# Slot arithmetic and two convolution additions placed on GpSimd in a Mamba-2 and mixture-of-experts kernel

## The chip, the cores and the metric

The kernel runs on one core of one Trainium2 chip. The metric is device time in microseconds from start to end of one execution; smaller is better.

## The reference

The input is x, 16 sequences of 512 tokens of 128 values, f32. The layer has two halves. The first is a Mamba-2 block: a projection of each token into z (256), xBC (512) and dt (4), a causal convolution with four taps over each of the 512 xBC channels, silu, and a scan in which a state of 4 heads x 64 x 128 is decayed and added to at each token. Its output is normalised by its root mean square, gated by silu(z), projected back to 128, added to x and layer-normalised. The second half is a mixture of 8 experts with the top 2 per token, again with residual and layer norm. Cut to what the change touches:

```python
xBC = conv1d(xBC, conv_w, 4 taps, causal) + conv_b     # each channel by itself
xBC = silu(xBC)                                        # 256 x channels, 128 B, 128 C
...
gates = sigmoid(u @ centroids.T); topk_vals, topk_idx = top_k(gates, 2)
gates = mask / sum(mask)
out = einsum('ne,end->nd', gates, outs)                # outs: each token by each expert
x = layernorm(x + out)
```

The kernel computes only the two chosen experts of a token. For that each token's row is written twice to a list in HBM that is sorted by expert.

## The kernel before, in words

The program has three stages. In the first the 16 sequences are walked in slots, written out one after another (`slots`, k from -1 to 16). In slot s the engines do three sequences at once: the scan of s, the projection and convolution of q = s+1, and the routing of r = s-1; the rows of s-2 are scattered to the list. A slot goes through four chunks c = 0..3 of 128 tokens. The second stage runs 136 tiles of 128 sorted rows through the experts, the third adds the two rows of each token and normalises. The order on each engine is the order of the code in `slot_pe`, `slot_act`, `slot_dve` and `slot_pool`; no scheduler moves anything, and each engine takes its instructions strictly in order, with semaphores between engines.

What matters in a slot, by engine and line:

- TensorE (`slot_pe`): per chunk the exponents (L420 to L425, into `pl`), transposes of xc (L518, L520), the state product (L524), a projection block for q (L399), the y products (L542, L548) and the new state (L556). In chunk 1 `turn_parts` (L412) and the transposes of the routed rows (L566). Behind the chunks: z, the sums of squares (L585), then the output product (L593), which waits for all four gated chunks (`g_ready`), the products of B and C (L496), z again (L407), the ranks (L609 to L613).
- ScalarE (`slot_act`): exponentials (L688), the copy `Btok` (L798), the convolution's newest tap with its bias (`tap0`, L730, into `acc`), in chunk 1 the normalised rows (L810), then `cur` (L719), `S` (L725, `keep_parts`), a square (L783) and the copy `uT` (L822). At the end silu of the four `acc` blocks (`activate`, L736).
- VectorE (`slot_dve`): `Xdt` (L1091), the statistics and `ve` (L1054), `carried`, `shift` (L1103), the masked `M` (L998), `yv` (L1117), `state` (L1122, L1125), and the other three taps of each of the four convolution blocks (`tap`, L924: acc += weight * shifted projection, read from PSUM). `take_ranks` and `place_rows` (L1002 to L1028) turn ranks into slot numbers: the product of picks and rows, its sum over 8 experts, the two gate values, two token numbers, a cast, and the next token numbers. They write the last two columns of `rowA` and `rowB`.
- GpSimd (`slot_pool`): `Xdd` (L1379), `decayed` (L1373), the gated chunk `gt` (`gate_y`, L1359), two powers (`rstd` L1394, `rms` L1415), and the eight indirect DMAs that scatter the rows of s-2 (L1366, four for `rowA`, four for `rowB`). Of the `rowA` scatters two stand behind gate_y(1), two behind gate_y(2); the four of `rowB` stand behind `rms`.

Waits of the lines quoted in the change: `Xdt` of chunk c < 3 waits for `Btok` of the same chunk; L556 waits for `Xdd`; L566 waits for `S` and for L810; L593 waits for gate_y(3).

Of the kernel before, what the change touches and what calls it, by code (L numbers as in the profile page):

```python
# [27 lines left out]
P = 128  # L28
# [20 lines left out]
G0 = 2  # L49
Q = 32  # L50
KS = 3 * Q
NH = NC * H
POS_STEPS = 4
# [24 lines left out]
def build(nc, t, out):  # L78
    ctx = ExitStack()
    with ctx:  # L80
# [6 lines left out]
        def sem(name):  # L87
# [31 lines left out]
        token_id = sb("token_id", [P, NC])  # L119
# [7 lines left out]
        acc = sb("acc", [P, XC, TOKS])  # L127
        xc = [sb(f"xc{i}", [P, XC, TOKS]) for i in range(2)]
# [33 lines left out]
        rowA = [sb(f"rowA{i}", [P, NC, ROW]) for i in range(2)]  # L162
        rowB = [sb(f"rowB{i}", [P, NC, ROW]) for i in range(2)]
# [11 lines left out]
        slotf = sb("slotf", [P, NC, 2])  # L175
# [34 lines left out]
              for big in (acc, xc[0]) for i in range(2)]  # L210
# [44 lines left out]
        names_pool = ("picks_made", "Xdd_ready", "decayed_ready", "g_ready", "rms_ready", "rstd_ready")
        (picks_made, Xdd_ready, decayed_ready, g_ready, rms_ready, rstd_ready) = [sem(n) for n in names_pool]
# [136 lines left out]
        def _(pe):  # L393
            def project_block(q, k):
                if k == 0:
                    wait(pe, sz_ready, CC * (q.n - 1) + 1)
                else:
                    wait(pe, conv_done, XC * q.n + k - 1)
                pe.matmul(pj[k % 2][:, :], w_xbc[:, k * P:(k + 1) * P], xT[:, q.n, :],  # L399
                          start=True, stop=True).then_inc(proj_psum, 1)  # L400

            def z_block(q, k):
                if k > 0:
                    wait(pe, carried_ready, (NC - 1) * q.n)
                else:
                    pe.wait_ge(conv_done, XC * q.n + 3)
# [93 lines left out]
            def slot_pe(s, scan, project, route):  # L500
# [4 lines left out]
                for c in range(NC):  # L505
                    tok = slice(c * P, (c + 1) * P)
                    n = NC * s.n + c
                    if scan and (c + 1 < NC or project):
# [26 lines left out]
                    if scan:  # L535
# [140 lines left out]
        def _(act):  # L676
# [50 lines left out]
            def tap0(q, c):  # L727
# [58 lines left out]
            def slot_act(s, scan, project, route):  # L786
# [4 lines left out]
                for c in range(NC):  # L791
# [94 lines left out]
        def _(dve):  # L886
# [115 lines left out]
            def take_ranks(r):  # L1002

                dve.wait_ge(rank_psum, r.n + 1)
                dve.tensor_tensor(rows[:, :, :], p4[:, 0:NC * E].rearrange("p (c e) -> p c e", e=E),
# [5 lines left out]

            def place_rows(r):

                link = chain(pos_step, POS_STEPS * r.n + 1)
                dve.wait_ge(rank_read, r.n + 1)
                dve.wait_ge(rowB_ready, r.n + 1)
                dve.reciprocal(gsum[:, :], gsum[:, :])
                link(dve.tensor_tensor(prow[:, :, :, :], picks[:, :, :, :],
                                       rows[:, :, :].unsqueeze(2).broadcast_to([P, NC, 2, E]), ALU.mult))
                link(dve.tensor_reduce(slotf[:, :, :], prow[:, :, :, :], AX_X, ALU.add))  # L1020
                for row, k in ((rowA, 0), (rowB, 1)):
                    dve.scalar_tensor_tensor(out=row[r.par][:, :, P + 1], in0=top[:, :, k], scalar=2.0,
                                             in1=gsum[:, :], op0=ALU.mult, op1=ALU.mult)
                    dve.tensor_scalar(row[r.par][:, :, P].bitcast(I32), token_id[:, :],
                                      float(TOKENS * k), None, ALU.add)
                link(dve.tensor_copy(slot[r.par][:, :, :], slotf[:, :, :]))
                dve.tensor_scalar(token_id[:, :], token_id[:, :], float(TOKS), None,
                                  ALU.add).then_inc(slot_ready, 1)  # L1028
# [27 lines left out]
            def slot_dve(s, scan, project, route):  # L1056
# [24 lines left out]
                for c in range(NC):  # L1081
# [50 lines left out]
                    if c == 1 and not (isinstance(s.n, int) and s.n < 2):  # L1132
                        place_rows(s.plus(-2))
# [9 lines left out]
                if route:  # L1143
# [4 lines left out]
                    wait_apart(dve, gate_step, gate + 2)  # L1148
                    for k in range(NC):
# [7 lines left out]
                if route:  # L1157
# [7 lines left out]
                    wait(dve, slot_ready, r.n)  # L1165
# [333 lines left out]
```

## Time and profile before

| | us |
|---|---|
| median of 3 runs (lowest, highest) | 817.68 (816.87, 819.04) |
| the profiled execution's own time | 816.69 |
| span of its instructions | 814.9 |
| busy: TensorE matmul | 667.5 |
| busy: VectorE | 617.5 |
| busy: ScalarE | 475.8 |
| busy: GpSimd | 433.0 |

How to read it: the span is shorter than the time by what lies around the first and the last instruction. Busy shares are means over the three stages. The walk over the sequences ends at about 450 us, the expert stage runs from about 480 to 780 us, the last stage fills the rest.

### The profile page before, as it was taken

How to read it: one execution, taken by the hardware profiler on the slowest of the kernel's cores; microseconds unless marked ns; L12 is line 12 of the kernel's file. 1: busy time of each engine (PE TensorE's matmuls, PEld its weight loads, DVE VectorE, ACT ScalarE, POOL GpSimd, SP SyncE). 2: the span in 40 equal slices, each digit the busy share in tenths (PEclk: the TensorE clock that was granted, in tenths of full speed). 3: DMA queues.
4: the chain of work that ended last, by engine and by line, in shares of the span. 5: the costliest groups of instructions: out<-in, count | busy, mean ns of one | idle time of the engine just before them, and what ended most of it. 6: DMA issues, size and time to landing. Idle time of an engine off the chain costs nothing.

```text
span 814.9 us, 21092 instructions
## 1 busy us (share of the span) xinstructions
PE 667.5 (82%) x5092; PEld 546.9 (67%) x5093; DVE 617.5 (76%) x2128; ACT 475.8 (58%) x1179; POOL 433.0 (53%) x498
## 2 busy tenths in 40 slices
PE   7969999888898898988987139999999999999300
PEld 5846666566665566655665129999999999999300
DVE  4398989889999899998896536666667666667485
ACT  3737766676766767667673115555555555556165
POOL 4023265656656566565756634555555555555464
PEclk9999999999999999999999559999999999999755
DMA  9160010111101111011100122222222222222496
GB/s 258 33 229 14 15 41 14 37 30 40 41 14 37 31 40 37 18 33 34 41 20 24 57 60 57 66 63 65 64 65 65 65 63 64 65 64 70 108 311 203
DMA packets 74801, 54.09 MB, mean 66 GB/s; under 512 B 9435, under 2 KB 70110, under 8 KB 74480
## 3 DMA queue, kind: packets, MB, share of 16 engines
q1 hardware_dynamic: 56400, 31.90, 14.9%
q0 software_dynamic: 8448, 16.93, 6.3%
q10 hardware_dynamic: 9888, 4.49, 2.0%
q8 instruction: 29, 0.48, 0.3%
q14 instruction: 36, 0.29, 0.1%
HBM read 31.11 MB, written 22.69 MB: 66 GB/s over the span
## 4 chain that ended last, share of the span: by engine, by line
PE 71%; issue 9%; ACT 7%; DVE 5%; POOL 3%; DMA 2%; ACTq 1%; SPq 1%; DVEq 0%; POOLq 0%
PE pl L633 16%; PE p L645 14%; PE pj L399 5%; PE p L585 4%; PE p L593 3%; PE p L542 3%; PE p L548 2%; PE pj L627 2%; ACT rowA L810 2%; ACT sz L872 2%; POOL sorted_rows L1366 2%; PE pj L407 2%; PE p L556 2%; PE p L496 2%; PE p L407 2%
## 5 line engine op out<-in xcount | busy, mean ns | idle before, releaser
L851 ACT ACTIVATE L<-pl,b_sb 128x128 f32<-128x128 f32 x544 | 155.4, 369 | 118.1 <-PE pl L633 118.1
L1428 POOL DMA_INDIRECT moe_rows<-yv,xs x136 | 145.7, 1072 | 140.5 <-DVE yv L1235 124.1
L633 PE MATMUL pl<-Btok,M 128*128 128x128 f32 x1088 | 151.7, 283 | 1.2 <-DVE M L1223 0.7
L924 DVE SCALAR_TENSOR_TENSOR acc<-pj,conv_w_sb,acc 128x511 f32<-128x511 f32 (+2 forms) x192 | 142.7, 743 | 4.0 <-ACT acc L730 1.1
L645 PE MATMUL p<-w,L 128*128 x1088 | 143.9, 275 | 1.3 <-ACT L L851 1.3
L633 PEld LDWEIGHTS pl<-Btok,M 128*128 128x128 f32 x1088 | 133.7, 193 | 4.3 <-DVE M L1223 1.4
L645 PEld LDWEIGHTS p<-w,L 128*128 128x128 f32 x1088 | 132.4, 192 | 1.8 <-issue 1.8
L1219 DVE COPY Btok<-pj 128x128 f32<-128x128 f32 x136 | 39.7, 292 | 78.2 <-PE pl L633 63.2
L1379 POOL TENSOR_TENSOR Xdd<-Xdt,cur 128x256 f32<-128x256 f32 x48 | 29.5, 615 | 88.0 <-DVE Xdt L1091 80.1
L1366 POOL DMA_INDIRECT sorted_rows<-rowA,slot x64 | 64.7, 1011 | 19.1 <-issue 17.0
L1366 POOL DMA_INDIRECT sorted_rows<-rowB,slot x64 | 62.7, 980 | 18.0 <-issue 18.0
L730 ACT ACTIVATE acc<-pj,conv_b_sb,conv_w_sb 128x512 f32<-128x512 f32 x64 | 49.5, 773 | 35.4 <-PE pj L399 35.3
L399 PE MATMUL pj<-xT,w_xbc 128*128 128x512 f32 x128 | 66.5, 601 | 0.0
L542 PEld LDWEIGHTS p<-M,Xdt 128*64 128x64 f32 x512 | 27.3, 136 | 52.5 <-issue 48.9
L627 PE MATMUL pj<-ident,xs 128*128 128x128 f32 x136 | 39.9, 294 | 23.3 <-DMA xs<-sorted_rows 20.8
L1223 DVE COPY M<-w 128x512 f32 x136 | 57.0, 419 | 0.0
L688 ACT ACTIVATE pl<-pl 128x512 f32<-128x512 f32 x64 | 37.3, 582 | 33.8 <-PE pl L425 33.2
L1359 POOL TENSOR_TENSOR gt<-yv,sz 128x256 f32<-128x256 f32 x64 | 47.0, 734 | 11.3 <-DVE yv L1117 10.6
L1235 DVE SCALAR_TENSOR_TENSOR yv<-yv,xs 128x128 f32<-128x128 f32 x136 | 47.8, 352 | 4.8
L1232 DVE TENSOR_TENSOR yv<-p,b2e_mem 128x128 f32<-128x128 f32 x136 | 39.5, 291 | 15.2 <-PE p L645 8.9
L542 PE MATMUL p<-M,Xdt 128*64 128x128 f32 x512 | 42.1, 284 | 9.5 <-issue 6.8
L998 DVE TENSOR_TENSOR M<-pl,Gm 128x512 f32<-128x512 f32 x64 | 43.8, 685 | 2.0 <-ACT pl L688 1.4
(204 smaller groups left out, 1341.7 us busy)
## 6 DMA issues: line engine op xcount, KB each, us to landing
xs<-sorted_rows SPq DMA_DIRECT2D x136, 65.0 KB, 1.8
xres<-in_x SPq DMA_DIRECT2D x16, 256.0 KB
w<-in_w SPq DMA_DIRECT2D x2, 2048.0 KB, 10.2
acc<-moe_rows SPq DMA_DIRECT2D x16, 256.0 KB, 4.2
xc<-moe_rows SPq DMA_DIRECT2D x16, 256.0 KB, 5.0
out<-sz ACTq DMA_DIRECT2D x16, 256.0 KB, 4.6
moe_rows<-yv,xs POOLq DMA_INDIRECT x136, 2.4
xc<-in_x SPq DMA_DIRECT2D x4, 256.0 KB, 5.1
```

Source lines behind the costliest of these rows:

```text
L399: pe.matmul(pj[k % 2][:, :], w_xbc[:, k * P:(k + 1) * P], xT[:, q.n, :], start=True, stop=True).then_inc(proj_psum, 1)
L542: mm = pe.matmul(p7[half, (h // 2) * P:(h // 2 + 1) * P], Xdt[c % 2][:, h * HD:(h + 1) * HD], M[c % 2][:, h, :], start=(h < 2), stop=(c == ...
L627: pe.transpose(pj[k % 2][:, 0:P], xs[k][:, 0:P], ident[:, :]).then_inc(sT_psum, 1)
L633: mm = pe.matmul(pl[k % 2][:, f * P:(f + 1) * P], w1e[k % 2][:, f * P:(f + 1) * P], sT[k % 2][:, :], start=True, stop=True)
L645: mm = pe.matmul(o[:, 0:P], hT[k % 2][:, f, :], w2[:, bass.ds(e, 1), f, :].rearrange("p e d -> p (e d)"), start=(f == 0), stop=(f == FB - 1))
L730: act.activation(acc[:, c, :], pj[c % 2][:, :], ACT.Identity, bias=conv_b[:, c:c + 1], scale=conv_w[:, c, TAPS - 1:TAPS]).then_inc(tap0_do ...
L851: act.activation(hT[k % 2][:, f, :], pl[k % 2][:, f * P:(f + 1) * P], ACT.Gelu, bias=b1[:, bass.ds(e * FB + f, 1)]).then_inc(hT_ready, 1)
L924: ins = dve.scalar_tensor_tensor(out=acc[:, k, j:TOKS], in0=pj[k % 2][:, 0:TOKS - j], scalar=conv_w[:, k, TAPS - 1 - j:TAPS - j], in1=acc[ ...
L1223: dve.tensor_copy(w1e[k % 2], w1[:, bass.ds(e, 1), :].rearrange("p e f -> p (e f)")).then_inc(w1e_ready, 1)
L1235: dve.scalar_tensor_tensor(out=ye[k % 4], in0=ye[k % 4], scalar=xs[k][:, P + 1:P + 2], in1=xs[k][:, 0:P], op0=ALU.mult, op1=ALU.add).then_ ...
L1366: pool.indirect_dma_start(out=sorted_rows[:, :], out_offset=bass.IndirectOffsetOnAxis(slot[q.par][:, c, k:k + 1], 0), in_=(rowA, rowB)[k][ ...
L1428: pool.indirect_dma_start(out=moe_rows[:, :], out_offset=bass.IndirectOffsetOnAxis(xs[k][:, P:P + 1].bitcast(I32), 0), in_=ye[k % 4], in_o ...
```

## The change

Five edits:

1. `place_rows` moves from VectorE to GpSimd. It becomes nine GpSimd instructions: twice the sum `gain`, the product of picks and rows, the sum over 8 experts as three halving additions (`half`), one product that writes both gate columns, one cast that writes both token columns, the cast to `slot`, and the next token numbers. `rowA` and `rowB` become the halves of one tensor `pair`. The reciprocal of `gsum` goes to `take_ranks`, which stays on VectorE.
2. For the two x blocks of the convolution (k < 2) the oldest tap leaves VectorE: ScalarE writes the product to `oldest[k]` right behind `tap0` (128x509), GpSimd adds it to `acc` (`add_oldest`, 128x509). `activate` of these blocks waits for the addition.
3. GpSimd's order in a slot: `place_rows(s-2)` stands behind gate_y(0), the first `rowA` scatter behind decay_state(2), `add_oldest(0)` and the other three `rowA` scatters behind gate_y(1), `add_oldest(1)` and the first `rowB` scatter behind gate_y(2), the other three `rowB` scatters behind `rms`.
4. On ScalarE `keep_parts` (S) moves ahead of the normalised rows in chunk 1, `set_current` (cur) to chunk 3.
5. On TensorE the exponents of chunk 2 move from the start of chunk 1 to a place ahead of the state product of chunk 0, behind its waits for `Btok` and `Xdd`.

```diff
@@ slot_pe
-                    if scan and (c + 1 < NC or project):
+                    if scan and c != 1 and (c + 1 < NC or project):
...
                             pe.wait_ge(Xdd_ready, (NC - 1) * s.n + c + 1)
                             if c == 0:
+                                exponents(s, 2)
                                 pe.wait_ge(sz_ready, CC * (s.n + 1))
@@ tap0
+                if c < BY_POOL:
+                    wait(act, oldest_added, BY_POOL * (q.n - 1) + c + 1)
+                    act.activation(oldest[c][:, TAPS - 1:TOKS], pj[c % 2][:, 0:TOKS - TAPS + 1], ACT.Identity,
+                                   scale=conv_w[:, c, 0:1]).then_inc(tap3_done, 1)
@@ slot_act
+                    if project and c == 1:
+                        keep_parts(q, p4[0:KS, 0:P])
...
-                    if project and c == 1:
+                    if project and c == 3:
                         set_current(q)
-                        keep_parts(q, p4[0:KS, 0:P])
@@ tap
+                on_dve = TAPS - 1 - (k < BY_POOL)
+                if j > on_dve:
+                    return
...
                 if j == 1:
                     dve.wait_ge(tap0_done, XC * q.n + k + 1)
+                    if k < BY_POOL:
+                        dve.wait_ge(tap3_done, BY_POOL * q.n + k + 1)
@@ on GpSimd
+            def place_rows(r):
...
+                pool.wait_ge(rows_ready, r.n + 1)
...
+                pool.tensor_tensor(gain[:, :], gsum[:, :], gsum[:, :], ALU.add)
+                link(pool.tensor_tensor(prow[:, :, :, :], picks[:, :, :, :],
+                                        rows[:, :, :].unsqueeze(2).broadcast_to([P, NC, 2, E]), ALU.mult))
+                part = prow
+                for k in range(3):
+                    w = E >> (k + 1)
+                    if k == 1:
+                        pool.tensor_tensor(pair[r.par][:, :, :, P + 1], top[:, :, 0:2].rearrange("p c k -> p k c"),
+                                           gain[:, :].unsqueeze(1).broadcast_to([P, 2, NC]), ALU.mult)
+                    if k == 2:
+                        pool.tensor_copy(pair[r.par][:, :, :, P].bitcast(I32), token_id[:, :, :])
+                    link(pool.tensor_tensor(half[k][:, :, :, :], part[:, :, :, 0:w], part[:, :, :, w:2 * w],
+                                            ALU.add))
+                    part = half[k]
+                link(pool.tensor_copy(slot[r.par][:, :, :], half[2][:, :, :, 0]))
+                pool.tensor_scalar(token_id[:, :, :], token_id[:, :, :], 1.0, float(TOKS), ALU.mult,
+                                   ALU.add).then_inc(slot_ready, 1)
+
+            def add_oldest(q, k):
+                pool.wait_ge(tap3_done, BY_POOL * q.n + k + 1)
+                pool.wait_ge(taps_read, XC * q.n + k + 1)
+                pool.tensor_tensor(acc[:, k, TAPS - 1:TOKS], acc[:, k, TAPS - 1:TOKS], oldest[k][:, TAPS - 1:TOKS],
+                                   ALU.add).then_inc(oldest_added, 1)
```

How the order moves, at three places of a slot in the middle of the walk. First GpSimd from `Xdd` of chunk 2 to the scatters behind `rms`, before:

```order
L1379 TENSOR_TENSOR Xdd<-Xdt,cur 128x256
L1359 TENSOR_TENSOR gt<-yv,sz 128x2x128
L1366 DMA sorted_rows<-rowA,slot 67584x130 x2
L1359 TENSOR_TENSOR gt<-yv,sz 128x2x128
L1366 DMA sorted_rows<-rowA,slot 67584x130 x2
L1359 TENSOR_TENSOR gt<-yv,sz 128x2x128
L1415 TENSOR_TENSOR rms<-ms,neg_half 128x4
L1366 DMA sorted_rows<-rowB,slot 67584x130 x4
```

and of the changed kernel:

```order
L1415 TENSOR_TENSOR Xdd<-Xdt,cur 128x256
L1359 TENSOR_TENSOR gt<-yv,sz 128x2x128
L1395 TENSOR_TENSOR acc<-acc,oldest 128x509
L1402 DMA sorted_rows<-pair,slot 67584x130 x3
L1359 TENSOR_TENSOR gt<-yv,sz 128x2x128
L1395 TENSOR_TENSOR acc<-acc,oldest 128x509
L1402 DMA sorted_rows<-pair,slot 67584x130
L1359 TENSOR_TENSOR gt<-yv,sz 128x2x128
L1462 TENSOR_TENSOR rms<-ms,neg_half 128x4
L1402 DMA sorted_rows<-pair,slot 67584x130 x3
```

Ahead of the last `gt` four scatters stand as before, in runs of three and one, and two additions are new.

Second, ScalarE from `Btok` of chunk 1 to `Btok` of chunk 2, before:

```order
L798 COPY Btok<-p 128x128
L810 ACTIVATE rowA<-rowA,shift,rstd 128x128 x4
L730 ACTIVATE acc<-pj,conv_b_sb,conv_w_sb 128x512
L719 COPY cur<-vals 128x80
L725 CAST S<-p 96x128
L783 ACTIVATE ysq<-yv 128x2x128
L822 COPY uT<-p 128x512
L688 ACTIVATE pl<-pl 128x512
L798 COPY Btok<-p 128x128
```

and of the changed kernel:

```order
L811 COPY Btok<-p 128x128
L731 CAST S<-p 96x128
L825 ACTIVATE pair<-pair,shift,rstd 128x128 x4
L736 ACTIVATE acc<-pj,conv_b_sb,conv_w_sb 128x512
L740 ACTIVATE oldest<-pj,conv_w_sb 128x509
L796 ACTIVATE ysq<-yv 128x2x128
L836 COPY uT<-p 128x512
L694 ACTIVATE pl<-pl 128x512
L811 COPY Btok<-p 128x128
```

`S` stands ahead of the four normalised rows, `cur` is gone from here, and one product is new.

Third, TensorE at the end of chunk 0, before:

```order
L542 MATMUL p<-M,Xdt 64x128 x4
L556 MATMUL p<-Xdd,Btok 128x256
L420 MATMUL pl<-too_early,ident_b 128x512
L422 MATMUL pl<-pick_s,S 128x512
L425 MATMUL pl<-S,pick_t 128x128 x4
L518 MATMUL p<-ident,xc 128x128 x2
```

and of the changed kernel:

```order
L547 MATMUL p<-M,Xdt 64x128 x4
L425 MATMUL pl<-too_early,ident_b 128x512
L427 MATMUL pl<-pick_s,S 128x512
L430 MATMUL pl<-S,pick_t 128x128 x4
L562 MATMUL p<-Xdd,Btok 128x256
L523 MATMUL p<-ident,xc 128x128 x2
```

The exponents of chunk 2 (`pl`) and the state product change places.

## Rows read from the trace of the kernel before

**Rows 1.** Windows view, a stretch of the walk: length; busy PE, PEld, DVE, ACT, POOL; clock.

```profile
136.00:300.00 164.00, 145.92 (x1038) 102.11 (x1037) 148.37 (x489) 113.83 (x220) 101.98 (x122) 1.00 0.12 34
```

**Rows 2.** Chain that ended last, pieces in order of time: start us, us, what.

```profile
54.22 0.67 DVE acc L924
...
248.21 1.32 issue
249.53 0.67 PE p L556 x2
```

**Rows 3.** Timeline of VectorE: start us, us, engine, line, what, idle before.

```profile
93.91 0.42 DVE L1091 TENSOR_TENSOR Xdt<-p,cur 128x256 f32<-128x256 f32 x1 [0.26 <-ACT Btok L798]
...
118.94 0.42 DVE L1091 TENSOR_TENSOR Xdt<-p,cur 128x256 f32<-128x256 f32 x1 [0.56 <-ACT Btok L798]
...
232.25 0.42 DVE L1091 TENSOR_TENSOR Xdt<-p,cur 128x256 f32<-128x256 f32 x1 [0.41 <-issue]
...
246.98 0.42 DVE L1091 TENSOR_TENSOR Xdt<-p,cur 128x256 f32<-128x256 f32 x1 [0.55 <-ACT Btok L798]
...
248.85 0.62 DVE L1054 TENSOR_SCALAR ve<-mv 128x4 f32<-128x4 f32 x1
...
257.86 0.42 DVE L1091 TENSOR_TENSOR Xdt<-p,cur 128x256 f32<-128x256 f32 x1 [0.41 <-issue]
...
426.89 0.42 DVE L1091 TENSOR_TENSOR Xdt<-p,cur 128x256 f32<-128x256 f32 x1 [0.56 <-ACT Btok L798]
...
428.61 0.17 DVE L1054 TENSOR_SCALAR ve<-mv 128x4 f32<-128x4 f32 x1
```

**Rows 4.** Timeline of GpSimd.

```profile
233.32 0.73 POOL L1359 TENSOR_TENSOR gt<-yv,sz 128x256 f32<-128x256 f32 x1
234.22 1.06 POOL L1366 DMA_INDIRECT sorted_rows<-rowA,slot  x1 [0.17 <-issue]
...
236.56 0.73 POOL L1359 TENSOR_TENSOR gt<-yv,sz 128x256 f32<-128x256 f32 x1
...
239.76 0.73 POOL L1359 TENSOR_TENSOR gt<-yv,sz 128x256 f32<-128x256 f32 x1
...
243.94 1.06 POOL L1366 DMA_INDIRECT sorted_rows<-rowB,slot  x1 [0.20 <-issue]
...
248.80 0.62 POOL L1379 TENSOR_TENSOR Xdd<-Xdt,cur 128x256 f32<-128x256 f32 x1
...
255.66 0.61 POOL L1373 TENSOR_TENSOR decayed<-state,cur 128x256 f32<-128x256 f32 x1 [2.11 <-DVE state L1125]
258.36 0.61 POOL L1379 TENSOR_TENSOR Xdd<-Xdt,cur 128x256 f32<-128x256 f32 x1 [2.09 <-DVE Xdt L1091]
...
454.49 1.03 POOL L1366 DMA_INDIRECT sorted_rows<-rowA,slot  x1 [2.14 <-DVE token_id L1027]
```

**Rows 5.** Timeline of TensorE, the output product.

```profile
241.74 1.98 PE L593 MATMUL p<-w_out,gt 128*128 128x128 f32 x16
```

**Rows 6.** Timeline of ScalarE, chunk 1 to chunk 2.

```profile
252.92 1.65 ACT L810 ACTIVATE rowA<-rowA,shift,rstd 128x128 f32<-128x128 f32 x4 [1.26 <-DVE shift L1103]
254.47 0.76 ACT L730 ACTIVATE acc<-pj,conv_b_sb,conv_w_sb 128x512 f32<-128x512 f32 x1
255.13 0.24 ACT L719 COPY cur<-vals 128x80 f32<-128x80 f32 x1
...
255.44 0.42 ACT L783 ACTIVATE ysq<-yv 128x256 f32<-128x256 f32 x1
256.40 0.59 ACT L822 COPY uT<-p 128x512 f32<-128x512 f32 x1 [0.55 <-PE p L566]
...
257.50 0.27 ACT L798 COPY Btok<-p 128x128 f32<-128x128 f32 x1
```

**Rows 7.** Groups of GpSimd instructions by shape: xcount, busy us, mean ns, idle before.

```profile
L1442 POOL TENSOR_TENSOR xc<-xc 128x128 f32<-128x128 f32 x8 | 3.6, 452 | 1.5 <-DMA xc<-moe_rows 0.8 <-ACT sz L872 0.7
...
L1347 POOL TENSOR_TENSOR which<-ident 96x16 f32<-96x16 f32 x1 | 0.2, 209 | 0.0
```

More of the change, by code:

```diff
@@ L49 @@
 G0 = 2
+BY_POOL = 2
 Q = 32
@@ L52 @@
 NH = NC * H
-POS_STEPS = 4
+POS_STEPS = 1
+PLACE_STEPS = 5
 FIN_STEPS = 3
@@ L127, in build @@
         acc = sb("acc", [P, XC, TOKS])
+        oldest = [sb(f"oldest{i}", [P, TOKS]) for i in range(BY_POOL)]
         xc = [sb(f"xc{i}", [P, XC, TOKS]) for i in range(2)]
@@ L161, in build @@
         shift = sb("shift", [P, NC])
-        rowA = [sb(f"rowA{i}", [P, NC, ROW]) for i in range(2)]
-        rowB = [sb(f"rowB{i}", [P, NC, ROW]) for i in range(2)]
+        pair = [sb(f"pair{i}", [P, 2, NC, ROW]) for i in range(2)]
+        rowA = [b[:, 0] for b in pair]
+        rowB = [b[:, 1] for b in pair]
         uT = sb("uT", [P, TOKS])
@@ L174, in build @@
         prow = sb("prow", [P, NC, 2, E])
-        slotf = sb("slotf", [P, NC, 2])
+        half = [sb(f"half{i}", [P, NC, 2, E >> (i + 1)]) for i in range(3)]
+        gain = sb("gain", [P, NC])
         slot = [sb(f"slot{i}", [P, NC, 2], I32) for i in range(2)]
@@ L397, in project_block @@
                 else:
-                    wait(pe, conv_done, XC * q.n + k - 1)
+                    wait(pe, taps_read, XC * q.n + k - 1)
                 pe.matmul(pj[k % 2][:, :], w_xbc[:, k * P:(k + 1) * P], xT[:, q.n, :],
@@ L1004, in take_ranks @@
                 dve.wait_ge(rank_psum, r.n + 1)
+                wait(dve, slot_ready, r.n)
                 dve.tensor_tensor(rows[:, :, :], p4[:, 0:NC * E].rearrange("p (c e) -> p c e", e=E),
@@ L1010, in take_ranks @@
                                   ALU.add).then_inc(rank_read, 1)
[L1012 to L1028, printed above, removed]
+                dve.reciprocal(gsum[:, :], gsum[:, :]).then_inc(rows_ready, 1)
             def residual(s):
@@ L1148, in slot_dve @@
                     wait_apart(dve, gate_step, gate + 2)
+                    wait(dve, slot_ready, r.n)
                     for k in range(NC):
@@ L1175, in _ @@
             take_ranks(Seq(0, SEQS - 1))
-            place_rows(Seq(0, SEQS - 1))
             link = chain(table_step, 0)
@@ L1387, in slot_pool @@
                     make_picks()
+                    for k in range(BY_POOL):
+                        add_oldest(q, k)
                     return
@@ L1398, in slot_pool @@
                     gate_y(s, 0)
+                if scatters:
+                    place_rows(old)
+                if scan:
                     decay_state(s, 2)
+                if scatters:
+                    scatter(old, 0, 0)
+                if scan:
                     decay_x(s, 2)
                     gate_y(s, 1)
+                if project:
+                    add_oldest(q, 0)
                 if scatters:
-                    scatter(old, 0, 0)
-                    scatter(old, 1, 0)
+                    for c in range(1, NC):
+                        scatter(old, c, 0)
                 if scan:
                     gate_y(s, 2)
+                if project:
+                    add_oldest(q, 1)
                 if scatters:
-                    scatter(old, 2, 0)
-                    scatter(old, 3, 0)
+                    scatter(old, 0, 1)
                 if scan:
@@ L1416, in slot_pool @@
                 if scatters:
-                    for c in range(NC):
+                    for c in range(1, NC):
                         scatter(old, c, 1)
             slots(pool, slot_pool)
+            place_rows(Seq(0, SEQS - 1))
             for k in range(2):
```

43 lines of the change are left out of this document (25 added, 18 removed).

## The prediction

> **What bounds the kernel now.** I read the windows view first. In a stretch in the middle of the walk VectorE is busy for 148.4 of 164 us and TensorE for 145.9, ScalarE for 113.8, GpSimd for 102.0, all at the full clock [rows 1]. So two engines are near their limit, GpSimd looks free, and the sum of busy time can't say more. The chain of waits then shows where TensorE stands still: 1.32 us before the state product of chunk 0 [rows 2], which waits for `Xdd`. GpSimd starts that `Xdd` at 248.80 only because the four `rowB` scatters that began at 243.94 stand ahead of it [rows 4]; `Xdt` was there at 247.40 [rows 3]. A second stop, from the end of the y products of chunk 1 to the transposes of the routed rows, ends with `S`, which stands on ScalarE behind the four normalised rows, the tap and `cur` [rows 6].
>
> Last I cut one period into three pieces, since a share over a slot hides who waits. The marks are `Xdt` of chunk 2 (232.25), the output product (241.74), `Xdt` of chunk 0 (246.98) and `Xdt` of chunk 2 again (257.86) [rows 3, 5]. B, from `Xdt` 2 to the output product, is 9.49 us; C, from there to `Xdt` 0, is 5.24; A, from `Xdt` 0 to `Xdt` 2, is 10.88. Together 25.61. From 118.94 to 426.89 there are 12 such periods, 25.66 on average [rows 3].
>
> **Piece A: a gain of 0.7 us.** With one of the four `rowB` scatters gone from ahead of it, `Xdd` 0 is ready 1.26 us earlier (four scatters take 4.86 from 243.94 to 248.80, the first 1.06 + 0.30 [rows 4]); so it no longer runs beside `ve`, which took 0.62 us in that company (248.85) and 0.17 in a slot where `Xdd` came a little later (428.61) [rows 3, 4]. The state product is also early enough. What VectorE does next in order, up to `shift`, comes 0.5 us earlier, less 0.08 for the reciprocal: 0.42. `S` and the exponents of chunk 2 then stand ahead of their users and cost nothing. ScalarE goes on behind `shift`: from the normalised rows (252.92) to `Btok` 2 (257.50) it now takes 4.58 us [rows 6]. The spacing behind `tap0` is 0.66 (254.47 to 255.13), and the new product, of the same form, adds this much. `cur` and `S` give back 0.31 (255.13 to 255.44). The copy `uT` came 0.96 after the square because the transposes were late (0.55 idle) [rows 6]; back to back it comes 0.31 after, so 0.65 more is saved. 4.58 + 0.66 - 0.31 - 0.65 = 4.28. Piece A: 10.88 - 0.42 - 0.30 = 10.16. The taps and the slot arithmetic that leave VectorE (about 2.5 us a slot) give nothing more here, since `Xdt` 2 waits for `Btok` 2 and the cover is ScalarE.
>
> GpSimd must still have `Xdd` 2 ready. Between gate_y(0) and `Xdd` 2 it has now 2.11 + 2.09 us idle [rows 4]; 0.3 of this goes, as piece A is shortened more at its end than at `shift`. `place_rows` goes in: nine instructions. The nearest row is 209 ns for 16 elements [rows 7]; with the slope below the nine take 1.9 us, and about 0.1 us at each of four waits on itself makes 2.3. The scatter that also goes in takes 1.25. 3.55 against 3.9: hidden, with only 0.35 us to spare. The low end of its cost is nothing; at the high end, if halving with short inner runs costs twice as much for each, it takes 3.5 and adds 0.85 us to each slot.
>
> **Piece B: a loss of 1.35 us.** Here GpSimd is given work on its only tight stretch. Before: `Xdd` 2 starts 0.50 us behind `Xdt` 2 (257.86 to 258.36), then gate_y(1), two scatters, gate_y(2), two scatters, gate_y(3), which ends at 240.49, 8.24 us behind `Xdt` 2, with no gap above 0.30 [rows 4]. The output product needs gate_y(3), and starts 1.25 us later [rows 5]. In the new order there are again four scatters in this stretch, and two additions of 128x509 besides. No row shows such an addition. The rows give 452 ns for 128x128 [rows 7] and 730 for 128x256 [rows 4]: 2.2 ns an element, so 1.29 us for 509. The low end comes from `Xdd` (615 ns, one operand repeated) and the 16-element row, 1.7 ns an element and 1.04 us; the high end adds 10% for strides, 1.42. I take 1.29, since both its rows have two full operands. Each addition overlaps its neighbour by 0.04, so the two take 2.50; gate_y(3) ends 10.74 behind `Xdt` 2, and the output product starts at 10.84 instead of 9.49. TensorE's own work would have let it start at 9.3.
>
> [...]
>
> **Piece C** keeps its order and its 5.24 us: the three `rowB` scatters left behind `rms` end 1 us before the next `Xdd`.
>
> A period: 10.16 + 10.84 + 5.24 = 26.24, 0.63 more than 25.61.
>
> **The sum.** Slots 3 to 14: 12 x 0.63 = +7.6. Slot 2 has scatters of `rowA` but none of `rowB` left over, and lasts 25.03 (93.91 to 118.94) [rows 3]; it goes to 26.24: +1.2. Slot 1 has no scatters, so GpSimd hides everything: 0. Slot 0 is carried by VectorE with its softplus steps between the taps (its tap on the chain costs 0.67 [rows 2]); two taps go: -1.3. In the startup ScalarE's new products stand ahead of copies that TensorE waits for; between nothing and one product of 0.7, and I take the latter: +0.7. At the end: slot 15 has no additions and keeps the 0.7 of piece A as a gain; behind its `rms` GpSimd carries the chain to its last scatter. One scatter has moved ahead (-1.26), the wait of 2.14 us for VectorE's slot arithmetic [rows 4] goes, and `place_rows` stands in twice, 2 x 2.45: together +1.5, less 0.7: +0.8. The table of tiles is built on VectorE beside the last eight scatters, as before. The expert stage and the last one hold no edited line. 7.6 + 1.2 - 1.3 + 0.7 + 0.8 = +9.0 us.
>
> The profiled execution took 816.69 us, so 825.7 for one like it. The median of the runs shown is 1.0 above it, so I predict 826.7.
>
> **Rivals.** (1) VectorE is the bound, and taking 2.5 us a slot from it counts. For it: 90% busy. Against it: piece B, where GpSimd had 1.25 us to spare and gets 2.5 us more. It decides where an addition takes under 0.9 us; then B is left to TensorE at 9.3, a period is 24.7, and 12 x -0.9 with slot 2 at -0.3 gives -11.1 + 0.2 from the ends: 807. Chance 0.12. (2) The additions take 1.04 us: each period is 0.5 shorter, 13 of them 6.5, and the time is 820; with a little more gain in piece A it can't be told from before. Chance 0.15. (3) `place_rows` takes 3.5 us or more on GpSimd: `Xdd` 2 is late by 0.85, and 13 slots give +11, the end +2: 840. The count of nine chained instructions speaks for it, the 209 ns row against it. Chance 0.13. My forecast keeps 0.60.
>
> **How the numbers follow.** A measurement of this kernel can tell 0.3%, 2.45 us, from no change. Within the forecast, additions of 1.42 us add 3.4, a `place_rows` of 3 us adds 6, and 0.35 us a slot more gain in piece A takes 4.5 off: 822 to 834. The range reaches down to 816, over rival 2 with that same gain, and up to 839, most of the way to rival 3; rival 1 stays outside. Faster 0.12, same 0.15, slower 0.73 (forecast and rival 3).
>
> **What the profile would show.** Right: VectorE's busy time down by some 45 us (32 taps and 16 times the slot arithmetic) and GpSimd's up by about 70 (32 x 1.29 and 16 x 1.9); the group of the addition at 1.26 to 1.29 us x32; the output product idle before, put down to gate_y on GpSimd, about 1.5 us in 13 slots; no stop before the state product of chunk 0; the period between two `Xdt` of chunk 0 near 26.2. Wrong: an addition under 1 us; the last gate_y of a slot ending before the sums of squares do; `Xdt` 2 less than 9.8 or more than 10.6 behind `Xdt` 0, in which case piece A is misjudged, through ScalarE or through `place_rows`.

## The result, and the profile after

The changed kernel takes **824.34 us** (median of 4 runs, 824.15 to 824.6), the kernel before, run beside it, 817.27 (816.5 to 819.04). The ratio is 1.0084, with a 95% interval of 1.0066 to 1.0101: slower by 7 us. The profiled execution has a span of 822.8 us (814.9 before).

The page of the changed kernel, busy time by engine and the chain that ended last:

```profile
span 822.8 us, 21204 instructions
PE 679.5 (83%) x5092; PEld 552.0 (67%) x5093; DVE 580.4 (71%) x1968; ACT 491.2 (60%) x1211; POOL 503.4 (61%) x674
...
PE 49%; POOL 25%; issue 14%; DVE 4%; ACT 3%; DMA 2%; SPq 1%; ACTq 1%; DVEq 0%; POOLq 0%
```

VectorE is 37 us less busy (45 were forecast), GpSimd 70 more (as forecast), and GpSimd now holds 25% of the chain, 3% before. The windows view of the stretch that [rows 1] showed:

```profile
136.00:300.00 164.00, 147.31 (x1023) 102.08 (x1023) 130.67 (x418) 117.64 (x228) 128.63 (x189) 1.00 0.10 32
```

No engine is above 90% here (the row has TensorE, its weight loads, VectorE, ScalarE, GpSimd), and VectorE has lost 18 us of work. The waits of TensorE in the same stretch say what holds it (waiting instruction, releaser: us in total, times, longest):

```profile
PE p L599 <- POOL gt L1359: 8.3, 7, 1.2
PE p L572 <- ACT pair L825: 3.2, 6, 0.5
PE p L529 <- DVE state L1125: 2.4, 6, 0.4
```

The output product (now L599) waits 1.2 us in each slot for GpSimd's last gate_y. The stop of 1.32 us before the state product of chunk 0 is gone. GpSimd's timeline in the middle of the walk answers to [rows 4]:

```profile
234.86 0.60 POOL L1415 TENSOR_TENSOR Xdd<-Xdt,cur 128x256 f32<-128x256 f32 x1 [0.26 <-DVE Xdt L1094]
235.43 0.72 POOL L1359 TENSOR_TENSOR gt<-yv,sz 128x256 f32<-128x256 f32 x1
236.11 1.26 POOL L1395 TENSOR_TENSOR acc<-acc,oldest 128x509 f32<-128x509 f32 x1
237.53 1.02 POOL L1402 DMA_INDIRECT sorted_rows<-pair,slot  x1 [0.16 <-issue]
...
241.10 0.74 POOL L1359 TENSOR_TENSOR gt<-yv,sz 128x256 f32<-128x256 f32 x1
241.78 1.28 POOL L1395 TENSOR_TENSOR acc<-acc,oldest 128x509 f32<-128x509 f32 x1
243.23 1.01 POOL L1402 DMA_INDIRECT sorted_rows<-pair,slot  x1 [0.17 <-issue]
244.26 0.74 POOL L1359 TENSOR_TENSOR gt<-yv,sz 128x256 f32<-128x256 f32 x1
...
250.93 0.61 POOL L1415 TENSOR_TENSOR Xdd<-Xdt,cur 128x256 f32<-128x256 f32 x1 [1.17 <-issue]
```

From `Xdd` 2 to gate_y(3) it never rests: an addition, three scatters, gate_y(2), an addition, a scatter, gate_y(3). In front of the next `Xdd` 0 it then has 1.17 us to spare, where the kernel before had none.

The marks of one period, on VectorE and (last row) TensorE, answer to [rows 3, 5]:

```profile
234.34 0.42 DVE L1094 TENSOR_TENSOR Xdt<-p,cur 128x256 f32<-128x256 f32 x1 [0.69 <-ACT Btok L811]
...
250.37 0.43 DVE L1094 TENSOR_TENSOR Xdt<-p,cur 128x256 f32<-128x256 f32 x1 [0.78 <-ACT Btok L811]
...
260.21 0.42 DVE L1094 TENSOR_TENSOR Xdt<-p,cur 128x256 f32<-128x256 f32 x1 [0.69 <-ACT Btok L811]
```

```profile
245.05 2.05 PE L599 MATMUL p<-w_out,gt 128*128 128x128 f32 x16 [1.20 <-POOL gt L1359]
```

So B is 10.71 us (before 9.49), C 5.32 (5.24), A 9.84 (10.88): a period of 25.87 where it was 25.61. The change gave A one microsecond and took 1.2 from B.

### The profile page after: what moved, and what is told of

Same layout as the page of the kernel before. It is cut to its first block, busy times and chain, and to the rows that moved or that the text cites. A ratio compares the mean times of both kernels' runs of the same rounds, so it can differ in the third digit from the quotient of the medians.

```text
span 822.8 us, 21204 instructions
## 1 busy us (share of the span) xinstructions
PE 679.5 (83%) x5092; PEld 552.0 (67%) x5093; DVE 580.4 (71%) x1968; ACT 491.2 (60%) x1211; POOL 503.4 (61%) x674
## 4 chain that ended last, share of the span: by engine, by line
PE 49%; POOL 25%; issue 14%; DVE 4%; ACT 3%; DMA 2%; SPq 1%; ACTq 1%; DVEq 0%; POOLq 0%
PE pl L639 16%; PE p L651 15%; POOL sorted_rows L1402 10%; POOL gt L1359 4%; PE p L599 4%; POOL acc L1395 3%; PE pj L633 2%; POOL rstd L1432 2%; PE p L501 2%; PE p L412 2%; ACT sz L886 2%; PE pl L448 2%; DVE st L1050 1%; DMA acc<-moe_rows 1%; PE pj L404 1%
## 5 line engine op out<-in xcount | busy, mean ns | idle before, releaser
L1402 POOL DMA_INDIRECT sorted_rows<-pair,slot x128 | 128.3, 1003 | 34.9 <-issue 33.4
L943 DVE SCALAR_TENSOR_TENSOR acc<-pj,conv_w_sb,acc 128x511 f32<-128x511 f32 (+2 forms) x160 | 118.7, 742 | 19.0 <-ACT oldest L740 15.6
L1094 DVE TENSOR_TENSOR Xdt<-p,cur 128x256 f32<-128x256 f32 x64 | 27.0, 422 | 32.7 <-ACT Btok L811 22.7
L599 PE MATMUL p<-w_out,gt 128*128 128x128 f32 x256 | 32.7, 281 | 16.0 <-POOL gt L1359 16.0
```

Of the source, the lines that this page charges most:

```text
L599: mm = pe.matmul(p5[:, c * P:(c + 1) * P], gt[:, k, c * P:(c + 1) * P], w_out[:, k, :], start=(k == 0), stop=(k == CC - 1))
L943: ins = dve.scalar_tensor_tensor(out=acc[:, k, j:TOKS], in0=pj[k % 2][:, 0:TOKS - j], scalar=conv_w[:, k, TAPS - 1 - j:TAPS - j], in1=acc[ ...
L1402: pool.indirect_dma_start(out=sorted_rows[:, :], out_offset=bass.IndirectOffsetOnAxis(slot[q.par][:, c, k:k + 1], 0), in_=(rowA, rowB)[k][ ...
```

## The experiments

All were timed beside the kernel before, whose medians on those chips were 816.1 to 816.8 us; each ratio is against that median. Each kernel is judged by the pieces A, B and C, read in the middle of its walk from the same three marks. The figures together, in us:

| kernel | time | A | B | C | period |
|---|---|---|---|---|---|
| before | 816.4 | 10.88 | 9.49 | 5.24 | 25.61 |
| changed | 824.3 | 9.84 | 10.71 | 5.32 | 25.87 |
| 1 no additions | 797.3 | 9.32 | 9.50 | 5.24 | 24.05 |
| 2 first `rowB` scatter back | 820.7 | 10.85 | 9.45 | 5.31 | 25.62 |
| 3 a third addition | 843.2 | 9.84 | 11.70 | 5.32 | 26.85 |
| 4 place_rows on VectorE | 818.9 | 9.84 | 10.76 | 5.32 | 25.90 |
| 5 as 1 and 4 | 807.6 | 9.85 | 9.84 | 5.24 | 24.95 |
| 6 before, edits 4 and 5 | 813.4 | 10.85 | 9.34 | 5.24 | 25.44 |
| 7 one addition | 801.4 | 9.32 | 9.84 | 5.31 | 24.46 |
| 8 before, edit 1 | 843.0 | 10.92 | 10.75 | 5.32 | 26.98 |
| 9 as 1, scatters as before | 812.9 | 10.39 | 9.49 | 5.24 | 25.12 |
| 10 gate_y(3) first | 804.6 | 9.84 | 9.35 | 5.33 | 24.52 |
| 11 as 1, last places on VectorE | 793.5 | 9.32 | 9.50 | 5.24 | 24.05 |
| 12 as 11, exponents as before | 794.3 | 9.32 | 9.50 | 5.24 | 24.06 |

**1. No additions.** The oldest taps go back to VectorE; all else stays.

```diff
-BY_POOL = 2
+BY_POOL = 0
...
-                if project:
-                    add_oldest(q, 0)
...
-                if project:
-                    add_oldest(q, 1)
```

> The changed kernel with no oldest tap on GpSimd: all four convolution blocks keep three taps on VectorE, ScalarE writes no product, GpSimd adds none; everything else as changed. Theory G (the two additions of 1.27 us each stand between Xdt 2 and gate_y(3), and GpSimd sets the output product there): piece B falls from 10.71 to TensorE's own 9.3 to 9.5, piece A from 9.84 to about 9.5 (ScalarE 0.6 shorter), C stays 5.3; a period of 24.1 to 24.5, so 800 to 806 us in all. Rival V (VectorE is the bound, the two taps it gets back cost 1.4 us a slot): the period stays at 25.8 or rises, 824 us or more. Rival P (the slot arithmetic on GpSimd is what costs): no gain, 822 to 826.

Measured: 797.26 us, ratio 0.9769 (0.9753 to 0.9786). That is 3 us below the range expected: B is as expected, and A is 9.32 where 9.5 was. The other four edits make the kernel 19 us faster, and edit 1 takes 27 us away again. VectorE as the bound (rival V) is refuted, since it got work back and the kernel became faster. TensorE's output product no longer waits; TensorE and VectorE are both above 90% busy, in the windows view of this kernel:

```profile
136.00:300.00 164.00, 156.49 (x1102) 108.06 (x1100) 149.74 (x462) 118.01 (x232) 121.77 (x193) 1.00 0.12 35
```

A also fell, by 0.52, with the products gone from ScalarE.

**2. The first `rowB` scatter back behind `rms`.**

```diff
-                if scatters:
-                    scatter(old, 0, 1)
                 if scan:
                     gate_y(s, NC - 1)
...
-                    for c in range(1, NC):
+                    for c in range(NC):
                         scatter(old, c, 1)
```

> The changed kernel with one scatter moved: the first rowB scatter, which stands ahead of gate_y(3), goes back behind rms, so that four stand there. The same work on every engine. Theory G: gate_y(3) ends 1.23 us earlier, piece B is 9.5, the next Xdd 0 is at most 0.2 us late and still early enough for the exponents; a period of 24.6 and 13 slots give -15: 808 to 811 us. Rival X (the delay of Xdd behind four scatters, 1.3 us in the kernel before, comes back in full): the period stays near 25.8, 824 us.

Measured: 820.72 us, ratio 1.005 (1.0032 to 1.0068). B fell by 1.26, as the scatter's price says, and A rose by 1.01. GpSimd's timeline in this kernel:

```profile
243.70 1.04 POOL L1460 TENSOR_TENSOR rms<-ms,neg_half 128x4 f32<-128x4 f32 x1 [1.04 <-DVE ms L1157]
244.94 1.05 POOL L1402 DMA_INDIRECT sorted_rows<-pair,slot  x1 [0.20 <-issue]
...
248.82 0.96 POOL L1402 DMA_INDIRECT sorted_rows<-pair,slot  x1 [0.30 <-issue]
249.80 0.63 POOL L1415 TENSOR_TENSOR Xdd<-Xdt,cur 128x256 f32<-128x256 f32 x1
```

and TensorE's, which stands 1.27 us for that `Xdd` before the exponents of chunk 2:

```profile
250.53 0.38 PE L425 MATMUL pl<-too_early,ident_b 128*128 128x512 bf16 x1 [1.27 <-issue]
```

Once gate_y(3) is early, `rms` waits for `ms` instead, so the four scatters behind it end no sooner, and `Xdd` 0 is late again. The scatter costs about the same on either side. The expectation of 808 to 811 us, by which the place ahead of gate_y(3) was the dear one, failed.

**3. A third addition** ahead of gate_y(3), on tiles of its own.

```diff
                     add_oldest(q, 1)
+                    pool.tensor_tensor(idle_out[:, TAPS - 1:TOKS], idle_in[:, TAPS - 1:TOKS],
+                                       idle_in[:, TAPS - 1:TOKS], ALU.add)
```

> The changed kernel with a third, useless addition of 128x509 on GpSimd behind add_oldest(1), that is ahead of gate_y(3), on tiles of its own. Theory G: 1.23 us more in piece B in each of 13 slots, +16, 840 us; slots 0 and 1 hide it. A rival by which GpSimd is not what the output product waits for: under +5, below 829.

Measured: 843.19 us, ratio 1.0338 (1.0303 to 1.0373). B rises by 0.99: GpSimd's queue in this piece is the bound there. Over 13 slots that is 13 us of the 19. The rest is TensorE's clock. Five of the 13 slots take 28.2 to 28.6 us instead of 26.85, 7.4 us in all (startup, slot 0 and end give 1.2 back), and in each of the five the output product runs slow after its stop:

```profile
225.46 3.48 PE L601 MATMUL p<-w_out,gt 128*128 128x128 f32 x16 [2.19 <-POOL gt L1362]
```

against 2.05 us in the changed kernel; the window around it has this granted clock (the third figure from the end), partly at the lower level, 1.2 GHz. The other eight slots had the same stop (2.17 to 2.25 us) and kept the full clock:

```profile
225.00:229.00 4.00, 3.54 (x19) 3.54 (x20) 0.85 (x5) 1.40 (x3) 3.42 (x4) 0.57 0.10 33
```

**4. place_rows back on VectorE**, at the end of chunk 1, in the changed kernel.

```diff
-                if scatters:
-                    place_rows(old)
...
                         take_ranks(s.plus(-2))
+                    if c == 1 and not (isinstance(s.n, int) and s.n < 2):
+                        place_rows(s.plus(-2))
```

> The changed kernel with place_rows back on VectorE, at the end of chunk 1, where VectorE waits 1.1 us for ScalarE's product; additions, scatters and the order of ScalarE and TensorE as changed. Theory G: pieces A and B unchanged (the arithmetic was hidden on GpSimd and is hidden on VectorE), period 25.9; behind slot 15 two times 3.2 us of GpSimd's chain go and 2.1 us of waiting come back, -4: 819 to 821 us. Rival P (the arithmetic costs GpSimd's chain in the walk too): 0.3 us or more a slot besides, 816 or less. Rival V: VectorE's 1.2 us come back in each slot, 835 or more.

Measured: 818.93 us, ratio 1.0039 (1.0025 to 1.0053). The period moves by 0.03: on GpSimd place_rows was hidden. Of the 5.4 us that are gained 3.4 lie at the end. From `Xdt` of slot 15 to the first expert matmul it is 51.90 us, and 55.31 in the changed kernel. Another 1.8 lie at the start of the expert stage, where the clock came back sooner (see below); no run ties that to this edit.

**5. Both of these.** 

> The changed kernel without the additions (edit 1) and with place_rows back on VectorE (edit 2): edits 3 to 5 alone. What it leaves out: nothing. Theory G (GpSimd ahead of TensorE is what costs; without the additions GpSimd has room, so place_rows there costs the period nothing, but costs 2.2 us twice in the last two slots, where nothing else hides it): periods as in the kernel without the additions (24.06, within 0.2), and 3 to 5 us less behind slot 14, so 793 to 796 us against its 797.3. Rival V (VectorE has become the bound at a period of 24: the 1.6 us of place_rows and the place it takes behind the row products of chunk 1 are then paid in each slot): periods 24.5 to 25, 803 to 810 us.

Measured: 807.64 us, ratio 0.9884 (0.9859 to 0.9908); rival V. Without the additions VectorE has no room: place_rows there costs 0.90 us a slot, in A and in B. So edit 2 earns nothing in the period beside edit 1, and 0.90 without it.

**6. The kernel before with the two orders (edits 4 and 5) alone.** 

> The kernel before with edits 4 and 5 alone: ScalarE copies S to cur behind block 3 and the parts at chunk 1, TensorE's exponents of chunk 2 go behind the wait for the scaled rows. Computes the same. If the orders are what brought the period of the kernel without the additions from 25.6 to 24.06: 24.1 to 24.6 here, 798 to 804 us. If the rest of it was needed (place_rows off VectorE, the scatters in ones and threes), so that in the kernel before the exponents only fall behind GpSimd's scaled rows, late by the two scatters ahead of it: 25.0 to 25.5, 809 to 815 us. Rival X: the exponents' wait is worth more than the copy's move: 25.8 or more, over 818 us.

Measured: 813.4 us, ratio 0.9959 (0.9945 to 0.9974). The period falls by 0.17, to 25.44, the second of the three cases expected. A hardly moves: the late `Xdd` 0 now holds up the exponents of chunk 2, before which TensorE stands 1.32 us.

**7. One addition**, block 0's (`BY_POOL = 1`, and the second call of `add_oldest` taken out). 

> The changed kernel with one addition in place of two: block 0's stays on GpSimd, block 1 has its oldest tap on VectorE as before. Computes the same. If each addition is paid in each slot alike (two cost 1.80 of period, a third 1.0): periods 24.95 to 25.05, 809 to 812 us. If the first one is free, since GpSimd has slack in front of gate_y(2), and the second pays for both: 24.1 to 24.4, 798 to 803 us. If the first one is what costs and the second is hidden: 25.6 or more, over 818 us.

Measured: 801.44 us, ratio 0.9807 (0.9785 to 0.9829). The first addition costs 0.41 us a slot, so it is not quite free, and the second 1.41. The second's price has two parts: 0.87 in B, where no slack is left, and 0.52 in A, which is block 1's product on ScalarE ahead of `Btok` 2. Block 0's product costs A nothing.

**8. The kernel before with edit 1 alone** (the changed kernel with place_rows, scatters and both orders as before). 

> The kernel before with edit 1 alone: the two additions on GpSimd, each ahead of gate_y(2) and gate_y(3), their products on ScalarE; place_rows on VectorE, the scatters in three twos and a two as before, the orders on TensorE and ScalarE as before. Computes the same. By my prediction's sum for edit 1 in piece B (2 x 1.29, less 0.65 of VectorE's time and the slack) this costs more than the whole change, which gave back by the scatter and the orders: periods 27.0 to 27.6, 838 to 850 us. If the additions' price does not depend on the rest (1.8 above the period without them): 27.2 to 27.5 where the other edits are worth 1.55, 842 to 848. Rival: the scatters' wait hides part, 26.2 to 26.8 and 826 to 836 us.

Measured: 842.96 us, ratio 1.0318 (1.0291 to 1.0345). Edit 1 by itself costs 26 us: 1.37 in the period, and, as in 3, some slots of 28.0 to 28.5 us. Here the clock falls after another stop:

```profile
215.46 1.09 PE L571 MATMUL p<-ident,pair 128*128 128x128 f32 x4 [2.17 <-ACT S L730]
...
214.00:218.00 4.00, 2.54 (x12) 1.96 (x13) 1.78 (x10) 2.36 (x7) 0.61 (x1) 0.66 0.00 0
```

That is the stop for `S`, which edit 4 shortens; with the product for block 1 ahead of `S` it is 2.17 us, and was at most 1.7 in the kernel before.

**9. As 1, with the scatters in twos as before.** 

> The changed kernel without the additions (edit 1) and with the scatters in twos as before (edit 3 undone); place_rows stays on GpSimd. Computes the same. Four scatters then stand ahead of slot s+1's first scaled rows again, the last of them ending 1.3 us after output product's start plus four, as in the run with the scatter moved back. Theory Q (GpSimd's queue ahead of the scaled rows of chunk 0 is paid as soon as TensorE has nothing else to wait for; the first scatter's move earned 1.0 us or more without the additions): periods 24.9 to 25.2, 808 to 813 us. Rival R (without the additions GpSimd is so far ahead that four scatters behind rms end in time): within 0.2 of 24.05, 796 to 800 us.

Measured: 812.89 us, ratio 0.9966 (0.9954 to 0.9978). A rises by 1.07: `Xdd` 0 is late again. Without the additions edit 3 is worth that much in every slot.

**10. gate_y(3) ahead of the second addition and the scatter.** Nothing is taken out.

```diff
+                if scan:
+                    gate_y(s, NC - 1)
                 if project:
                     add_oldest(q, 1)
                 if scatters:
                     scatter(old, 0, 1)
                 if scan:
-                    gate_y(s, NC - 1)
                     pool.wait_ge(ms_ready, s.n + 1)
```

> The changed kernel with one thing reordered on GpSimd: gate_y(3) ahead of block 1's addition and of the scatter behind it (in the changed kernel it comes after both). All the work stays. Computes the same. Theory Q (an addition costs by what it stands ahead of, gt(3) and through it the output product; behind gate_y(3) it costs only what Silu of block 1 then waits): output product without a wait for gt, periods 24.4 to 24.9, 802 to 809 us. Rival L (GpSimd's load as such bounds the period: 22 us of work and issue gaps in a slot, so an addition moved later pushes rms, the scatters and the scaled rows of the next chunk 0 back by the same): 25.4 to 25.9, 818 to 825 us.

Measured: 804.58 us, ratio 0.9857 (0.9837 to 0.9877). This is the run that decides. GpSimd does all that it does in the changed kernel, its order differs at one place, and 20 us are gone, 17.4 in slots 2 to 14 and 2.6 in slot 0:

```profile
231.75 1.42 POOL L1359 TENSOR_TENSOR gt<-yv,sz 128x256 f32<-128x256 f32 x2
233.11 1.27 POOL L1395 TENSOR_TENSOR acc<-acc,oldest 128x509 f32<-128x509 f32 x1
234.55 1.01 POOL L1402 DMA_INDIRECT sorted_rows<-pair,slot  x1 [0.17 <-issue]
235.59 1.05 POOL L1463 TENSOR_TENSOR rms<-ms,neg_half 128x4 f32<-128x4 f32 x1
...
240.41 0.63 POOL L1415 TENSOR_TENSOR Xdd<-Xdt,cur 128x256 f32<-128x256 f32 x1
```

gate_y(2) and gate_y(3) come together, the addition and the scatter fill the time in which `rms` would wait, and `Xdd` 0 starts 0.74 us behind `Xdt` 0 (239.67). TensorE's output product starts without a wait:

```profile
234.34 1.98 PE L599 MATMUL p<-w_out,gt 128*128 128x128 f32 x16
```

Rival L, GpSimd's load as such, is refuted. But the additions still don't pay: run 1, without them, is 7 us faster, mostly by the 0.52 that block 1's product costs in A.

**11. As 1, with place_rows of the last two sequences on VectorE**, the other 14 on GpSimd. 

> The kernel without the additions, with place_rows of the last two sequences on VectorE and the other 14 on GpSimd. Computes the same. Against the kernel without the additions (797.3): behind slot 14 place_rows and the wait behind it are what GpSimd's last 16 scatters wait for; the runs with all of place_rows on VectorE reached the expert stage 51.9 us after slot 15's first rows, those with it on GpSimd 55.3 to 55.5. So the stage starts 3 to 3.5 us earlier, and TensorE's clock comes back as soon: 792.5 to 795 us, periods unchanged at 24.05. Rival: the 3.4 us came from something else in those two kernels (the statistics of the last sequences): under 1 us, 796 to 798.

Measured: **793.53 us**, ratio 0.9726 (0.9708 to 0.9743), 23 us below the kernel before; with run 12, which can't be told from it, the fastest of all. The first expert matmul comes 52.10 us behind slot 15's `Xdt`, 55.51 in run 1.

**12. As 11, with the exponents of chunk 2 at the head of chunk 1 again.** 

> The fastest kernel so far (no additions, place_rows of the last two sequences on VectorE; 793.5 us, period 24.05) with edit 5 undone on TensorE: the exponents of chunk 2 stand at the head of chunk 1 again and not ahead of chunk 0's state product. Computes the same. Theory T (edit 5 paid only where the scaled rows came late; here they are ready 0.1 us before the exponents start, so the 0.65 us of exponents only push the state product, and TensorE then stands 0.39 us for the state that comes of it): 0.3 to 0.5 us less in each period, 23.6 to 23.75, 787 to 790 us. Rival U (the piece from the first rows of chunk 0 to those of chunk 2 is carried by VectorE's statistics and shift, then ScalarE's four normalised rows, whatever TensorE does): 24.0 to 24.1, 792 to 795 us. Rival W (the exponents then reach ScalarE too late for chunk 2's mask): 24.3 or more, over 797.

Measured: 794.33 us, ratio 0.9725 (0.971 to 0.9739), the period 24.06: rival U. Edit 5 earns nothing here. Edit 4 was never undone alone, so what it is worth by itself stays open.

## Why the prediction was right, and where its sum was not

The time, 824.34, lies 2.4 us from the 826.7 forecast, and the mechanism was the one named: the additions go into the one stretch where GpSimd had no room, TensorE's output product waits for gate_y(3), and a gain in A pays most of it back. But the sum came near by errors that cancel. Against the span of the kernel before:

| part | predicted | measured |
|---|---|---|
| startup and slot 0 | -0.6 | +1.5 |
| slot 1 | 0 | -0.3 |
| slot 2 | +1.2 | +0.9 |
| 12 slots | +7.6 | +2.4 |
| slot 15 to the expert stage | +0.8 | +0.8 |
| expert stage, clock at its start | 0 | +1.9 |
| the rest | 0 | +0.7 |
| all | +9.0 | +7.9 |

**Piece B** was forecast at 10.84 and is 10.71. The group of the addition by shape (count, busy us, mean ns; 112 to 424 us):

```profile
L1395 POOL TENSOR_TENSOR acc<-acc,oldest 128x509 f32<-128x509 f32 x25 | 31.7, 1269 | 0.0
```

1.27 us for 1.29 taken; rival 2 (1.04 us) is out. No row stood behind the 1.26 at the low end of the sign; the mean is 1.269. The stop was 1.2 us, not 1.5. The Trainium skill's page GPSIMD Engine Reference (section Elementwise — side-by-side cycle accounting) states about 2.6 cycles an element for a two-input `tensor_tensor`, an estimate of 2.2 ns at the 1.2 GHz it reckons with. The trace agrees: from gate_y with 256 elements (0.734 us) to the addition with 509 (1.269) it is 2.1 ns an element.

**Piece A** failed by size: 9.84 for 10.16, and this 0.32 in 12 slots is 3.8 of the 5.2 us by which the periods were over-estimated. The step from the normalised rows to `Btok` 2, forecast at 4.28, took 4.07. ScalarE's timeline, which answers to [rows 6]:

```profile
255.78 1.65 ACT L825 ACTIVATE pair<-pair,shift,rstd 128x128 f32<-128x128 f32 x4 [0.20 <-DVE shift L1106]
257.34 0.76 ACT L736 ACTIVATE acc<-pj,conv_b_sb,conv_w_sb 128x512 f32<-128x512 f32 x1
258.00 0.67 ACT L740 ACTIVATE oldest<-pj,conv_w_sb 128x509 f32<-128x509 f32 x1
258.57 0.41 ACT L796 ACTIVATE ysq<-yv 128x256 f32<-128x256 f32 x1
258.87 0.57 ACT L836 COPY uT<-p 128x512 f32<-128x512 f32 x1
...
259.85 0.27 ACT L811 COPY Btok<-p 128x128 f32<-128x128 f32 x1
```

The product takes its place in 0.57 us, not 0.66, and the exponents follow the copy after 0.47, where I had the 0.60 of the kernel before. The rows up to the normalised ones came 0.1 us sooner too. The rest is 1.6 from B (0.13 in each slot), 0.6 from setting one undisturbed period, 25.61, against a walk whose 12 periods average 25.66, less the 0.9 that C took more than forecast (5.32 for 5.24). **place_rows**, 2.3 us by the forecast, spans 2.22 (256.37 to 258.59), and run 4 shows it hidden; rival 3 is out.

**Startup and slot 0** are the step that failed: slot 0 grew by 1.4 us (29.44 to 30.84) where I had -1.3, and the startup by 0.1 where I had +0.7. I took the -1.3 us of the two taps as certain, because the chain ran over VectorE there. Two things took it. First, VectorE's softplus steps beside GpSimd's work, in the changed kernel (VectorE, then GpSimd):

```profile
55.55 0.68 DVE L987 TENSOR_SCALAR tail<-L 128x224 f32<-128x224 f32 x1
56.27 1.33 DVE L989 SCALAR_TENSOR_TENSOR vals<-b2e_mem,tail 128x224 f32<-128x224 f32 x1
```

```profile
55.23 0.87 POOL L1359 TENSOR_TENSOR gt<-yv,sz 128x256 f32<-128x256 f32 x1
56.07 1.28 POOL L1395 TENSOR_TENSOR acc<-acc,oldest 128x509 f32<-128x509 f32 x1
```

and without the additions (run 1):

```profile
56.39 0.28 DVE L987 TENSOR_SCALAR tail<-L 128x224 f32<-128x224 f32 x1
56.70 0.39 DVE L989 SCALAR_TENSOR_TENSOR vals<-b2e_mem,tail 128x224 f32<-128x224 f32 x1
```

The first step ran beside gate_y(2), the second beside the addition. TensorE's stop before the next y products is 2.44 us in the changed kernel, 1.36 before and in run 1. In runs 2, 4 and 8, where the second addition falls on the same steps, they take 0.68 and 1.33 again and the stop is 2.44 or 2.45; in run 7, with one addition, 0.28, 0.39 and 1.36; in run 10, where it comes later, 0.68, 0.39 and 1.51. So the 1.33 is the second addition's doing, and the 0.68 is not. There slot 0 takes 28.23 us, 1.2 less than before: the gain that I forecast, once the second addition is out of the way. Second, the clock after that stop, in the changed kernel:

```profile
60.00:64.00 4.00, 4.00 (x15) 2.90 (x14) 3.86 (x8) 2.23 (x3) 0.73 (x1) 0.57 0.02 4
```

and 1.00 before. The two pairs of matmuls of the running sums took 0.95 us each for 0.54, the z product behind them 1.79 for 1.02: 1.6 us on the path.

**The expert stage** was forecast unchanged. It starts 5.3 us later, but its sixth scatter comes 7.2 us later (506.93 for 499.75). In the windows view of the changed kernel TensorE, after 23.03 us of rest, gets the full clock back only from 498 us on:

```profile
490.00:494.00 4.00, 3.22 (x15) 2.93 (x15) 0.86 (x3) 3.45 (x9) 0.00 (x0) 0.50 0.28 68
494.00:498.00 4.00, 4.00 (x25) 4.00 (x24) 1.65 (x6) 1.14 (x4) 0.99 (x1) 0.63 0.04 15
498.00:502.00 4.00, 4.00 (x38) 4.00 (x37) 2.96 (x12) 2.28 (x8) 1.79 (x2) 1.00 0.14 35
```

before, it was at 0.92 in the second window of the stage (486 to 490). Which condition brings it back stays open: run 2 rested as long (23.13) and lost nothing here (18.38 us from its first matmul to the sixth scatter; 18.36 before, 20.22 in the changed kernel). In all fourteen traces this piece takes either 18.3 to 18.5 us (nine) or 20.0 to 20.2 (the changed kernel, runs 3, 5, 8 and 10), with rests of 20 and of 23 us in both groups. Executions of the kernel before lie up to 4 us apart (815.1 to 819.0) without any edit. So no run shows that the change caused these 1.9 us, and that they brought the total near the forecast is luck.

**Rival 1** put the kernel at 807, with a period of 24.7, if an addition took under 0.9 us. Run 1 shows that I undervalued what lies under edit 1: with no addition at all the period is 24.05. I had forecast A at 10.16, so never saw that edits 2 and 3 hold each other up. The orders alone have 25.44 (run 6), so the pair gains 1.39; undone alone from run 1, one costs 1.07 (run 9) and the other 0.90 (run 5), together more than the pair gains. The forecast asked only whether the change as a whole pays. Its own terms, 1.35 lost in B and 0.72 gained in A, already said that one edit of five spends what the others earn.

## What to carry to other kernels

Price work moved to a free-looking engine by what stands behind it in that engine's order until the next waiter is served, and not by busy share. The same addition cost 0.4 us a slot ahead of a gate with slack, 1.4 ahead of the one that TensorE waited for, with its product, and about nothing in B behind that gate: move such work behind before judging it. Then still compare with leaving it out, since the product that the addition needs from ScalarE has a price too: here 804.6 us moved behind, 797.3 left out. And take a bundle of edits apart: here edits 2 to 5 earned 19 us, and edit 1 hid it.

## What the hardware did that I had not expected

- A VectorE operation on two SBUF inputs stretched beside a GpSimd addition of two SBUF inputs: 128x224 in 1.33 us for 0.39 (and the next step in 1.10 for 0.39 beside the third addition of run 3). A one-input step of 128x224 took 0.68 for 0.28 beside gate_y(2), in run 10 as well, where no addition stood there. The Trainium skill's page SBUF — State Buffer (section Who interferes with whom) says that a VectorE instruction with two SBUF inputs contends with a GpSimd one that reads SBUF; the trace agrees for the two-input steps. The taps, whose product comes from PSUM, kept 0.74 us.
- TensorE's granted clock fell to the lower level after stops of 2.0 to 2.4 us within the walk (runs 3 and 8, slot 0 of the changed kernel). The stop's length alone does not decide: run 3 stood 2.17 to 2.29 us in each of 13 slots and the clock fell in five; it stood 3.15 us in slot 0, and the window behind it was at 1.00. Its third addition, 0.99 us in B, so cost about 2.4 us in each of those five slots.
